# First absorbed attention: the product of probabilities and folded values as three float16 products instead of one float32 product

## The reference

```python
q_big = jnp.einsum('bshk,hkq->bshq', q_hk, w_kc_q)       # 192 wide
q_big = _apply_rope(q_big, sin_q, cos_q)
kv_r = _apply_rope(kv_c, sin_k, cos_k)
q_r = jnp.einsum('bshq,hqr->bhsr', q_big, W_qr)
k_r = jnp.einsum('bld,hdr->bhlr', kv_r, W_kr)
scores = jnp.einsum('bhsr,bhlr->bhsl', q_r, k_r)
attn = jax.nn.softmax(scores, axis=-1)
ctx_c = jnp.einsum('bhsl,bld->bhsd', attn, kv_r)
ctx_lat = jnp.einsum('bhsd,hkd->bhsk', ctx_c, w_kc_kv)
ctx = ctx_lat.transpose(0, 2, 1, 3).reshape(Bv, Sv, H * K)
return ctx @ Wo.T
```

## Time and profile before

| what | value |
|---|---|
| runs shown | 1290.97, 1292.52, 1293.19 us (median 1292.52) |
| profiled execution | 1289.97 us |
| its span | 1288.1 us |
| PE busy | 1187.8 us, 92% of the span |
| DVE busy | 878.0 us, 68% |
| ACT busy | 509.2 us, 40% |
| POOL busy | 377.6 us, 29% |
| granted TensorE clock, mean | 0.979 |

### The profile page before, as it was taken

How to read it: one execution, slowest core, us unless ns; L and a number is a source line. 1 busy time by engine, 2 the same in 40 slices (tenths; PEclk the granted TensorE clock), 3 DMA queues, 4 the chain that set the end, 5 groups by cost and what they waited for, 6 DMA issues and landing times.

```text
span 1288.1 us, 21896 instructions
## 1 busy us (share of the span) xinstructions
PE 1187.8 (92%) x8466; PEld 772.8 (60%) x8483; DVE 878.0 (68%) x1713; ACT 509.2 (40%) x1141; POOL 377.6 (29%) x393
## 2 busy tenths in 40 slices
PE   6889999999789999999899888989999888899997
PEld 3654558999545556655566545554556555465565
DVE  3777967667366666666757687887666666766666
ACT  3423360111124344334353235753343353555553
POOL 1540216565203333333203320001333342233332
PEclk9898999999889999999999999999999989999999
DMA  4030140000145444444330000001543200333442
GB/s 145 2 155 21 48 157 23 1 2 2 47 152 132 122 115 115 115 115 119 106 139 1 1 17 2 2 2 34 139 116 119 83 18 2 89 115 115 121 130 83
DMA packets 41544, 97.20 MB, mean 75 GB/s; under 512 B 5446, under 2 KB 18246, under 8 KB 39392
## 3 DMA queue, kind: packets, MB, share of 16 engines
q1 hardware_dynamic: 41440, 95.79, 24.8%
HBM read 94.35 MB, written 1.42 MB: 74 GB/s over the span
## 4 chain that ended last, share of the span: by engine, by line
PE 73%; DVE 16%; ACT 4%; issue 3%; POOL 2%; DMA 1%; SPq 0%; DVEq 0%; POOLq 0%; ACTq 0%
PE PS L1404 10%; PE PS L1405 10%; PE PS L1406 10%; PE PS L1449 4%; PE PS L1451 4%; PE PS L1450 4%; PE PS L1039 3%; PE PS L1057 2%; PE PS L1223 2%; ACT arena L2200 2%; PE PS L1025 2%; PE PS L1027 2%; PE PS L1026 2%; PE PS L2123 1%; DVE small L550 1%
## 5 line engine op out<-in xcount | busy, mean ns | idle before, releaser
L1625 POOL TENSOR_TENSOR arena<-arena,m_g 128x512 f32<-128x512 f32 x142 | 183.1, 1291 | 412.0 <-DMA m_g<-gate_rows 244.0
L1404 PE MATMUL PS<-arena 128*128 128x512 f16 x608 | 231.2, 380 | 2.8 <-DVE arena L1560 2.8
L1405 PE MATMUL PS<-arena 128*128 128x512 f16 x608 | 231.0, 380 | 0.0
L1406 PE MATMUL PS<-arena 128*128 128x512 f16 x608 | 230.8, 380 | 0.0
L1449 PE MATMUL PS<-arena 128*128 128x256 f16 x608 | 165.8, 273 | 11.0 <-DVE arena L1580 8.3
L1451 PE MATMUL PS<-arena 128*128 128x256 f16 x608 | 165.7, 273 | 0.0
L1450 PE MATMUL PS<-arena 128*128 128x256 f16 x608 | 165.7, 273 | 0.0
L1520 ACT ACTIVATE arena<-PS 128x512 f32<-128x512 f32 x112 | 66.9, 597 | 244.5 <-PE PS L1406 234.1
L1563 DVE SCALAR_TENSOR_TENSOR arena<-arena,PS 128x512 f32<-128x512 f32 x112 | 77.0, 687 | 124.7 <-ACT arena L1520 124.3
L1580 DVE TENSOR_TENSOR arena<-arena 128x512 f16<-128x512 f32 x142 | 110.1, 776 | 3.6 <-ACT arena L1530 3.6
L1406 PEld LDWEIGHTS PS<-arena 128*128 128x128 f16 x608 | 59.6, 98 | 72.2 <-issue 0.8
(11 more groups left out here) (282 smaller groups left out, 2256.9 us busy)
## 6 DMA issues: line engine op xcount, KB each, us to landing
w_stage<-in_up SPq DMA_DIRECT2D x80, 256.0 KB, 2.9
m_g<-gate_rows SPq DMA_DIRECT2D x70, 256.0 KB, 4.2
arena<-in_heads SPq DMA_DIRECT2D x16, 1088.0 KB, 5.3
w_stage<-in_down SPq DMA_DIRECT2D x80, 128.0 KB, 4.0
m_g<-gate_rows SPq DMA_DIRECT2D x17, 512.0 KB, 3.9
m_g<-gate_rows SPq DMA_DIRECT2D x6, 448.0 KB, 4.1
m_g<-gate_rows SPq DMA_DIRECT2D x6, 384.0 KB, 4.5
m_g<-gate_rows SPq DMA_DIRECT2D x6, 320.0 KB, 4.1
```

Of the source, the lines that this page charges most:

```text
L1404: pe.matmul(to, w_hi, x_hi, start=(k == 0), stop=False)
L1405: pe.matmul(to, w_lo, x_hi, start=False, stop=False)
L1406: ins = pe.matmul(to, w_hi, x_lo, start=False, stop=(k == KT - 1))
L1625: pool.tensor_tensor(m_c[:, st % 2, :], m_b[:, st % LAG, :], m_g[:, st // 2 % 2, st % 2, :], ALU.mult).then_inc(s.c, 1)
```

## The change

The output's product is no longer a float32 matmul. Probabilities and F are each split in a high float16 part (64 times the value, rounded) and a low one (64 times the value minus the high part), and three float16 products (high·high, high·low, low·high) are accumulated; the factor is taken out in the addition to x.

The parts that matter below:

```diff
 # fold: ACT writes the high part where it wrote float32, one count for two copies
-                    act.activation(fold_f[:, c::2, q, :], PS[:, f_banks(q)[c], :].rearrange("p (b c) -> p b c", b=2),
-                                   ACT.Copy).then_inc(s.f, 1)
+                    ins = act.activation(rot_f[:, 0, c::2, q, :], PS[:, f_banks(q)[c], :].rearrange("p (b c) -> p b c", b=2),
+                                         ACT.Copy, scale=SPLIT)
+                ins.then_inc(s.f, 1)
...
 # fold: DVE gets the low part
+            def values_low(q):
+
+                dve.wait_ge(s.f, 2 * q + 1)
+                for c in range(2):
+                    hi, lo = (rot_f[:, a, c::2, q, :] for a in range(2))
+                    ins = dve.scalar_tensor_tensor(lo, PS[:, f_banks(q)[c], :].rearrange("p (b c) -> p b c", b=2), SPLIT, hi,
+                                                   ALU.mult, ALU.subtract)
+                ins.then_inc(s.f, 1)
...
             placed(0)
+            values_low(0)
             low(1)
...
                 placed(q - 1)
                 if 0 <= q - 3 < NT // 2:
                     turned(q - 3)
+                values_low(q - 1)
             placed(PAIRS - 1)
+            values_low(PAIRS - 1)
...
 # PE: bank 6 is free, and the output may start, when DVE's low part is done
                 if b or e:
-                    pe.wait_ge(soft.t, ROT_0 + 4 * b + e)
+                    pe.wait_ge(soft.low, 4 * b + e)
...
             def output(b, q):
-                pe.wait_ge(soft.t, ROT_0 + 4 * b + 2 + q + 1)
+                pe.wait_ge(soft.low, 4 * b + 2 + q + 1)
...
-                    ins = pe.matmul(PS[:, out_bank(b, q), 0:D], at_pt[:, q, j * P:(j + 1) * P], fold_f[:, b, j, :],
-                                    start=(j == 0), stop=(j == PAIRS - 1))
+                    pe.matmul(to, p_hi, f_hi, start=(j == 0), stop=False)
+                    pe.matmul(to, p_hi, f_lo, start=False, stop=False)
+                    ins = pe.matmul(to, p_lo, f_hi, start=False, stop=(j == PAIRS - 1))
...
 # ACT: the copy of bank 6 writes the high part (scale=SPLIT)
 # DVE, rotations
-                dve.tensor_tensor(tile, tile, PS[:, out_bank(b, q), 0:D], ALU.add).then_inc(soft.x, 1)
+                dve.scalar_tensor_tensor(tile, PS[:, out_bank(b, q), 0:D], UNSPLIT, tile, ALU.mult, ALU.add).then_inc(soft.x, 1)
...
+            def low(b, e):
+                half, q = EVENTS[e]
+                hi, lo = (rot_pt[:, q, a, half * 512:(half + 1) * 512] for a in range(2))
+                dve.wait_ge(soft.t, ROT_0 + 4 * b + e + 1)
+                dve.scalar_tensor_tensor(lo, PS[:, 6, :], SPLIT, hi, ALU.mult, ALU.subtract).then_inc(soft.low, 1)
+
             for g in range(ROT_END):
+                for e in range(4):
+                    if at_turn(g, TURN_AT[e] + 1) is not None:
+                        low(at_turn(g, TURN_AT[e] + 1), e)
                 if g < UNITS:
                     rotated(g)
```

More of the change, by code:

```diff
@@ L170, in build @@
         at_pt, at = take(at, [2, 1024])
+        rot_pt = at_pt.rearrange("p q c -> p (q c)").bitcast(F16).rearrange("p (q a c) -> p q a c", q=2, a=2)
         tables = [xn.rearrange("p t c -> p (t c)")[:, t * 4 * S:(t + 1) * 4 * S] for t in range(2)]
@@ L203, in build @@
         ln_xT_before = {0: 0, 2: 4, 4: 8, 6: 12}
-        soft = Sems("soft", "sub p sums t_ps t y_ps x")
+        soft = Sems("soft", "low sub p sums t_ps t y_ps x")
         turns_before = {n: 2 * NT * n for n in range(4)}
@@ L210, in build @@
                2: Sems("att2", "w0 w1 bt_ps bt e_ps e m_ps mh m f_ps f c_ps c dt_ps dt q s")}
-        pre = [Sems("pre0", "w fold_ps fold ms r z zT_ps zT biased y_ps ssq rr z2 z2T_ps h low"),
+        pre = [Sems("pre0", "w fold_ps fold ms r z zT_ps zT biased y_ps ssq z2 z2T_ps h low"),
                Sems("pre1", "w h low logit e t"),
                Sems("pre2", "w hT z zT_ps ms r qkv biased copied qr qrT_ps qhi qT s mx p pt_ps pt one oneT_ps oneT v pv o y_ps x2 "
-                    "ssq rr z2 z2T_ps h low logit e t"),
+                    "ssq z2 z2T_ps h low logit e t"),
                Sems("pre3", "w h low logit lg t")]
@@ L601, in build @@
         fold_f = at_f.rearrange("p (b j c) -> p b j c", b=B, j=PAIRS)
+        rot_f = at_f.bitcast(F16).rearrange("p (a b j c) -> p a b j c", a=2, b=B, j=PAIRS)
         W_KCQ, W_Q, W_KV, W_O, W_KR, W_QR = 0, 256, 512, 576, 832, 896
@@ L1056, in output @@
                 for j in range(PAIRS):
-                    ins = pe.matmul(PS[:, out_bank(b, q), 0:D], at_pt[:, q, j * P:(j + 1) * P], fold_f[:, b, j, :],
-                                    start=(j == 0), stop=(j == PAIRS - 1))
+                    to, (p_hi, p_lo) = PS[:, out_bank(b, q), 0:D], (rot_pt[:, q, a, j * P:(j + 1) * P] for a in range(2))
+                    f_hi, f_lo = (rot_f[:, a, b, j, :] for a in range(2))
+                    pe.matmul(to, p_hi, f_hi, start=(j == 0), stop=False)
+                    pe.matmul(to, p_hi, f_lo, start=False, stop=False)
+                    ins = pe.matmul(to, p_lo, f_hi, start=False, stop=(j == PAIRS - 1))
                 ins.then_inc(soft.y_ps, 1)
@@ L1087, in evacuated @@
                     act.wait_ge(soft.y_ps, NT + 2 * b - 1 + q)
-                act.activation(at_pt[:, q, half * 512:(half + 1) * 512], PS[:, 6, :], ACT.Copy).then_inc(soft.t, 1)
+                act.activation(rot_pt[:, q, 0, half * 512:(half + 1) * 512], PS[:, 6, :], ACT.Copy, scale=SPLIT).then_inc(soft.t, 1)
             for g in range(ROT_END):
@@ L1770, in pool_pre0 @@
                 pool.tensor_tensor(p0_h[:, i, :], xn[:, i, :], p0_bias, ALU.add).then_inc(s.biased, 1)
-            pool_pow(pre[0].ssq, 1, rms_r[:], rms_e[:], pre[0].rr)
+            pool_pow(pre[0].ssq, 1, rms_r[:], rms_e[:], pre[0].r)
             nc.gpsimd.wait_ge(pre[0].low, NT // 2)
@@ L1819, in dve_pre0 @@
             dve.tensor_scalar(rms_e[:], p0_ssq, 1.0 / D, RMS_EPS, ALU.mult, ALU.add).then_inc(s.ssq, 1)
-            dve.wait_ge(s.rr, 1)
+            dve.wait_ge(s.r, 2)
             for i in range(NT):
@@ L2300, in pool_pre2 @@
             pool_values(me)
-            pool_pow(pre[2].ssq, 1, rms_r[:], rms_e[:], pre[2].rr)
+            pool_pow(pre[2].ssq, 1, rms_r[:], rms_e[:], pre[2].r)
         def dve_pre2():
```

## The result

The changed kernel took 1303.3 us in the median of 6 runs (1299.34 to 1307.16) against 1292.12 (1289.71 to 1293.56) of the kernel before: a ratio of 1.0087, interval 1.0070 to 1.0104, so 11.2 us slower. The profiled execution took 1303.71 us (span 1301.9).

What follows compares the result with a forecast made beforehand. PE was taken to bound the rotations, with waits between engines deciding the fold and tail. 7.0 - 5.0 + 2.9 + 2.7 = +7.6 us on the median 1292.52 gave 1300.1 us, 0.6% slower; range 1295 to 1304.

Steps and rivals of the forecast that it cites:

- the clock rival: TensorE's clock falls to half at the fold's end, losing 1.7 or 3.4 us; result about 1302.5; chance 0.15.
- the three terms: One per stretch: fold +7.0, rotations 5.0 saved and 2.9 lost, tail net +2.7; sum +7.6 us.
- The fold, +7.0: Fold: VectorE's new low-part work delays keys, last waits and start; 3.6 + 2.7 + 0.5 + 0.2 us.
- The pair at 1.29 us: Fold: two low-part instructions of 128x512 on VectorE, priced at 1.29 us, bounds 1.02 to 1.38.
- the period 5.88: Fold: keys were forecast to come every 5.9 us, not 4.98, idle about 0.9 until VectorE's new product.
- the first wait: Start of the fold: a pair put into VectorE's 0.76 us idle time makes its next work 0.5 us late.
- the two last waits: End of fold: waits ahead of last keys and first query last until VectorE's pair is done; 2.7 us together.
- The rotations, -5.0 + 2.9 = -2.1: Rotations: six shorter outputs save 5.0 us on PE; a late low part in each of three batches loses 2.9.
- the 0.95: Rotations: event 1's low part at the head of unit 15 makes PE's later transposes 0.95 us late per batch.
- The tail, +4.4 - 1.7 = +2.7: Tail: maxima wait behind low parts, transposes come 3.7 and finally 4.4 us late; two shorter outputs save 1.7.
- The rivals that put the loss elsewhere: Fold half hidden: 1296.6, chance 0.13; PE's saving wins: 1290.2 or 1285.8, chances 0.06 below 1289.9, 0.08 up to 1295.1.
- the free 10.8 us of VectorE in the fold: Fold: rivals' ground that VectorE's idle 10.8 us could absorb the eight new pairs, 10.3 us in all.

Runs made afterwards that it cites:

- rotations-only: Products-only variant (three float16 products, no low parts made) with low parts of the probabilities restored in the rotations, folded values' left out; ratio 1.0000 to the kernel before.
- both orders: Changed kernel with low values earlier and PSUM banks released singly in the fold, plus reordered copies and low parts in the rotations; ratios 0.9976 and 0.9965 to before.
- single-part kernels: Two kernels, each with three float16 products but low parts made only for folded values or only for probabilities; ratios 1.0006 and 1.0000 to before.
- released fold: Changed kernel with low values ahead of x's low part, PSUM released bank by bank and the last wait moved to scores of unit 6; ratio 1.0011 to before.
- before, warm: Kernel before the change, with useless matmuls filling gaps ahead of the last keys and behind the tail's transposes; ratio 1.0017 to the kernel before.
- fold-only: Products-only variant (three float16 products, no low parts made) with low parts of the folded values restored, probabilities' left out; ratio 1.0006 to the kernel before.
- rotation-order kernel: Changed kernel with ScalarE copying bank 6 ahead of the exponential and VectorE's low parts at the ends of units; ratio 1.0042 to the kernel before.

## Why the prediction was right, and where it was short

The sign, the mechanism and the range held (1303.3 in 1295 to 1304); the middle, 1300.1, was 3.2 us low. That the number lay inside, 0.7 us from the upper end, is owed to the clock rival, which that end had in it, and not to the three terms.

- The fold, +7.0: 6.86 in the two kernels with low values and full clock in the fold. The pair at 1.29 us (1.28), the period 5.88, the first wait 0.5 longer (1.05 to 1.53) and the two last waits 1.32 longer each (1.30 to 2.62, 1.41 to 2.73) all came as summed.
- The rotations, -5.0 + 2.9 = -2.1: -2.64 at full clock (rotations-only). The stall was 0.86 a batch for my 0.95, and with no stall the saving is 5.23 (both orders). VectorE's product of unit 15 was late as summed, but the 0.95 was put on the transposes of unit 18: 0.70 of the 0.86 fell ahead of the scores of units 17 and 18, on GpSimd's additions, and 0.16 was left for the transposes.
- The tail, +4.4 - 1.7 = +2.7: +2.80 in rotations-only, +4.2 - 1.4 by the two kernels with one kind of low parts each. Counted from the first transposes, the third and fourth came 3.5 and 4.3 later than before, for 3.7 and 4.4.
- These make 7.0 us. The other 3.9 are the clock: the changed kernel against the same stretches at the clock of the single-part kernels, 48.28 - 46.52 = 1.76 in the fold, 133.05 - 131.80 = 1.25 in the first units of the rotations, 22.47 - 21.56 = 0.91 in the tail. 7.0 + 3.9 = 10.9.

The step that fell short is the sentence "By the rows alone it is open, as both gaps are near that stretch's idle share; so it is a rival, not a term", with a chance of 0.15. The row it rested on had PE busy 1.43 of 3.4 us ahead of the fall, and about the same share came here: 1.48 of 3.4, then 0.50. I had the added waits and the bursts between them, and so could have worked out how little TensorE would do there. The rival's own result, 1302.5, was within 1 us of the measurement, in part by luck: it had 2.4 us for the clock, where 3.9 were lost, 0.9 of them in the tail, and the three terms together were 0.6 too high. The argument against it, that short bursts lie between the gaps, is what the rows refute.

The low end of the range, 1295, follows only with all of the 2.9 us of the rotations left out (7.6 - 2.2 - 2.9 over 1292.5); with half of it left out, as the text can be read, it would be 1296.5.

The rivals that put the loss elsewhere fell: the free 10.8 us of VectorE in the fold did not hide the pairs until they were put in the right place, and released bank by bank, and then nearly all of their time was hidden.

## What to carry to other kernels

Moving work to an engine with free time helps only if the work lands in the free time: ask what stands ahead of it in that engine's order, what it waits for, and which wait ends on it. Here the same arithmetic cost 11 us in one order and gave 3 to 4.5 us in another, with the waits set closer to what they guard. And sum idle time on TensorE per stretch, not per gap: two added waits that each look harmless can be followed by half the clock, and the price falls on matmuls that the change never touched.

## What the runs showed of the hardware that I had not expected

- The half clock lasted 10.2 us in the changed kernel though PE was busy 6.77 us of them, and 13.7 us in the tail with 6.77 busy. I had priced one or two stretches of 3.4 us. The Trainium skill's page "TensorE: Matmul & The Clock Gate", section "Why this matters for your kernels", speaks of idle gaps above some length; here the clock fell 1.9 us into the gap of 2.62 us (194.97 to 196.9), behind a stretch in which PE was partly busy (1.48 of 3.4), and in the tail 0.3 us into a gap of 5.75 us (1.56 of 3.4). In the released fold, two shorter gaps (2.02 and 1.23 us) left the clock at 1.00. The half clock can stay though TensorE has work all the time: in the trace of before, warm it was busy 17.0 of 17.0 us at 0.50 (782 to 799).
- Where it falls differs between kernels with the same two waits of 2.62 and 2.73 us: from 196.9 in the changed kernel, at a cost of 1.76 + 1.25 = 3.0 us, and from 203.1 in the fold-only one, whose keys and values at the end ran at full clock, at a cost of 1.1 (130.30 against 129.21 in both orders). The rotation-order kernel, with the changed one's fold, has the changed one's loss (48.27). No kernel in which the clock fell there was traced twice, so how much this varies from execution to execution is not shown.
- PE stalls of 0.16 to 0.38 us, as those of the rotations, leave no idle time in the timeline's brackets; the starts of like groups show them.
